# Decay exponentials of a chunked recurrent layer grouped into wider activations, with the split of w moved into the sub-tile loop

## What is computed

```python
w_ = -jnp.exp(w_)                      # decay, from a small projection of h1
wc = jnp.cumsum(w, axis=-2)            # inside chunks of 32 tokens
kw = k * jnp.exp(wc[..., -1:, :] - wc)
S  = S * d[..., None] + kv             # state, chunk after chunk
qe = q * jnp.exp(wc - w)
ke = k * jnp.exp(-wc)
A  = jnp.where(mask, qe @ ke.T, 0.0)
o  = o_inter + A @ v + diag[..., None] * v
out = (groupnorm(o) * silu(g)) @ o_w.T
h = silu(x @ wg.T) * (x @ wu.T); ffn = h @ wd.T
```

## Time and profile before

| | us |
|---|---|
| median of 5 runs | 4532.4 |
| the runs | 4475.2, 4484.1, 4532.4, 4586.9, 4603.8 |
| the profiled execution, slowest core | 4484.1 |
| its span, first to last instruction, core 2 | 4482.5 |
| outside the span | 1.6 |
| spans of the eight cores | 4436.0 to 4482.5 |

### The profile page before, as it was taken

The page is one execution under the profiler, slowest core; times in us unless marked ns, Lnnn a source line. Parts: engine busy times, 40 slices in busy tenths (PEclk is TensorE's granted clock), DMA queues, the critical chain, the costliest instruction groups (busy, mean ns, idle before and its releaser), DMA issues.

```text
span 4482.5 us, 35856 instructions; the slowest of 8 cores (4436.0 to 4482.5 us)
## 1 busy us (share of the span) xinstructions
PE 2154.6 (48%) x11249; PEld 968.6 (22%) x11424; DVE 1449.0 (32%) x2844; ACT 1423.8 (32%) x1552; POOL 300.7 (7%) x525
## 2 busy tenths in 40 slices
PE   0387224762257621675317752187332873248622
PEld 0132111321123211232102321032111321113211
DVE  0230442314432143321433224331343314523144
ACT  0342423323233332333323333243323323324241
POOL 1010000100001000110001000010000100001000
PEclk9998567985679756887558965598656986569856
DMA  9545004540235302443024420254103541044500
GB/s 156 102 80 93 6 12 83 87 78 5 39 69 87 64 5 52 71 82 54 10 52 71 82 50 10 56 85 77 36 10 66 94 74 26 10 75 76 94 5 15
DMA packets 88440, 257.76 MB, mean 58 GB/s; under 512 B 10206, under 2 KB 10527, under 8 KB 84639
## 3 DMA queue, kind: packets, MB, share of 16 engines
q0 software_dynamic: 83088, 221.82, 29.7%
q1 hardware_dynamic: 5168, 33.62, 3.4%
...
## 4 chain that ended last, share of the span: by engine, by line
PEldq 21%; DVE 20%; issue 16%; DMA 14%; ACT 11%; PEld 7%; ACTq 5%; another core or an unknown queue 3%; DVEq 2%; POOL 1%; POOLq 0%; SPq 0%
PEldq L285 20%; ACT L146 10%; DMA sb_fu<-w_fu 7%; ACTq L151 5%; DVE sb_qg L146 4%; DMA sb_x<-x 4%; DMA sb_vgo<-w_g 3%; DVE sb_z L146 3%; DVE sb_gst L146 2%; DVE sb_S L146 2%; DVE sb_o L146 2%; DVE sb_xin L146 1%; DVEq L144 1%; PEld Po L741 1%
## 5 line engine op out<-in xcount | busy, mean ns | idle before, releaser
L146 ACT ACT_TABLE_LOAD x704 | 903.2, 1283 | 3022.7 <-PEq L285 2100.7
L1180 PE MATMUL PtrT<-sb_id,sb_z 128*128 128x128 bf16 x256 | 32.4, 306 | 660.3 <-DVEq L151 660.3
L407 PE MATMUL PtrT<-sb_id,sb_xnt 128*128 128x128 bf16 x256 | 32.4, 306 | 513.1 <-DVEq L151 373.9
L146 DVE COPY sb_gff<-PtrT 128x512 bf16<-128x512 bf16 x64 | 27.2, 425 | 738.4 <-PEq L285 738.4
L577 PE MATMUL Pa<-sb_xnT,sb_fg 128*128 128x512 bf16 x738 | 191.9, 402 | 81.4 <-DMA sb_fu<-w_fu 36.0
L577 PE MATMUL Psm<-sb_xnT,sb_fg 128*128 128x512 bf16 x752 | 178.0, 378 | 61.8 <-DMA sb_fu<-w_fu 37.2
L146 DVE SCALAR_TENSOR_TENSOR sb_hall<-Pb,sb_scr 128x512 bf16<-128x512 f32 x96 | 66.4, 692 | 435.8 <-ACTq L151 431.3
L459 PE MATMUL Pb<-sb_hall,sb_fd 128*128 128x512 bf16 x746 | 201.3, 431 | 9.8 <-issue 9.0
L557 POOL DMA_DIRECT2D sb_fg<-w_fg x192 | 108.9, 567 | 1439.6 <-PEq L285 1400.5
L146 DVE TENSOR_SCALAR sb_qg<-sb_qe,sb_G 128x32 bf16<-128x32 bf16 x768 | 179.9, 234 | 74.4 <-ACTq L151 10.2
L459 PE MATMUL Pa<-sb_hall,sb_fd 128*128 128x512 bf16 x750 | 192.3, 416 | 9.6 <-issue 9.0
...
## 6 DMA issues: line engine op xcount, KB each, us to landing
sb_fg<-w_fg POOLq DMA_DIRECT2D x192, 256.0 KB, 4.0
sb_fu<-w_fu POOLq DMA_DIRECT2D x192, 256.0 KB, 4.8
...
```

The costliest lines, as they stand in the source:

```text
L146: return fn(*a, **k)
L407: e.transpose(Ptr[:, c * 128:(c + 1) * 128], sb_xnt[:, 0, c * 128:(c + 1) * 128], sb_id[:])
L1180: e.transpose(Ptr[:, c * 128:(c + 1) * 128], sb_z[:, c * 128:(c + 1) * 128], sb_id[:])
```

## The change

Four things are done together.

1. The five argument groups of a sub-tile become three. G1 holds qe and kw: 16 matmuls into Pw, one exponential of 1024 columns into sb_ex, two products. G2 holds qt and ks in the same way, through Pab, one tensor that joins Pa and Pb. K holds ke alone (its exponential has the other sign): 8 matmuls into Pa and 512 columns into sb_scr. sb_ex doubles in size.
2. G1 waits for `Supd`, the end of the state update, because that update reads Pw; K waits for G2's exponential, which reads Pab.
3. The w matmul, exponential and split of a sub-tile (`rA`) are no longer made for all four ahead of the stage. That of sub-tile 0 stands there, that of ts + 1 between `rC1(ts)` and `rC2(ts)`. The halves lie in sb_whi and sb_wlo, one sub-tile at a time, and use only Pb and sb_scr.
4. The select becomes a memset of sb_mt and a predicated copy onto it; sb_zero goes.

```diff
-    sb_ex = A("sb_ex", [128, 2, NH * 128], BF16)
+    sb_ex = A("sb_ex", [128, 2, 2 * NH * 128], BF16)
...
-    Pa = nc.alloc_psum_tensor("Pa", [128, 512], F32)
-    Pb = nc.alloc_psum_tensor("Pb", [128, 512], F32)
+    Pab = nc.alloc_psum_tensor("Pab", [128, 1024], F32)
+    Pa = Pab[:, 0:512]
+    Pb = Pab[:, 512:1024]
...
         rB1(it, 0)
         rB2(it, 0)
         for ts_ in range(NST):
             rC1(it, ts_)
+            if ts_ + 1 < NST:
+                rA(it, s, m, ts_ + 1)
             rC2(it, ts_)
             if ts_ + 1 < NST:
                 rB1(it, ts_ + 1)
...
+    def rA(it, s, m, ts_):
+        def pw2_t(e, en, ts_=ts_):
+            en.w(cs, ev["h1"])
+            en.w(cs, st["qk_free"])
+            en.w(cs, st["pb_free_s"])
+            if ts_ > 0:
+                en.w(cs, st["argB_free"])
+            e.matmul(Pb[:, 0:512], sb_h1[:, ts_ * 128:(ts_ + 1) * 128],
+                     sb_ww2[:, :], start=True, stop=True)
+            ev[f"w2t{ts_}"] = sig_t(e)
+        on("tensor", pw2_t)
...
+        def pw2_s(e, en, ts_=ts_):
+            en.w(ct, ev[f"w2t{ts_}"])
+            if ts_ == 0:
+                en.w(ct, ev[f"gft{NC-1}"])
+            else:
+                en.w(cv, ev[f"facK_{ts_-1}"])
+            e.activation(out=wf_ap, in_=Pb[:, 0:512], func=AF.Exp)
+            ev[f"wexp{ts_}"] = sig(e, cs)
+        on("scalar", pw2_s)
...
+        def pw2_v(e, en, ts_=ts_):
+            en.w(cs, ev[f"wexp{ts_}"])
+            if ts_ > 0:
+                en.w(ct, ev[f"gt{ts_-1}"])
+            e.tensor_copy(out=sb_whi[:].rearrange("p h t -> p (h t)"), in_=wf_ap)
+            e.tensor_tensor(out=sb_wlo[:].rearrange("p h t -> p (h t)"),
+                            in0=wf_ap,
+                            in1=sb_whi[:].rearrange("p h t -> p (h t)"),
+                            op=ALU.subtract)
+            ev[f"wsp{ts_}"] = sig(e, cv)
+        on("vector", pw2_v)
...
+        def pG1_t(e, en, ts_=ts_):
+            en.w(cv, ev[f"wsp{ts_}"])
+            en.w(cv, st["Supd"])
+            if ts_ == 0:
+                en.w(cs, ev["pvg4_3"])
+            for h in range(NH):
+                e.matmul(Pw[:, h * 128:(h + 1) * 128], sb_whi[:, h, :],
+                         sb_mqe[:], start=True, stop=False,
+                         skip_group_check=True)
+                e.matmul(Pw[:, h * 128:(h + 1) * 128], sb_wlo[:, h, :],
+                         sb_mqe[:], start=False, stop=True,
+                         skip_group_check=True)
...
+            ev[f"argG1_{ts_}"] = sig_t(e)
+        on("tensor", pG1_t)
...
+        def pG1_s(e, en, ts_=ts_):
+            en.w(ct, ev[f"argG1_{ts_}"])
+            en.w(cv, st["exp_rd"][0])
+            e.activation(out=sb_ex[:, 0, :], in_=Pw[:, :], func=AF.Exp,
+                         bias=0.0, scale=-1.0)
+            ev[f"gx1_{ts_}"] = sig(e, cs)
+        on("scalar", pG1_s)
...
+        def pG2_t(e, en, ts_=ts_):
+            en.w(cv, ev[f"wsp{ts_}"])
+            if ts_ == 0:
+                en.w(cs, st["pa_free_s"])
+                en.w(cs, st["pb_free_s"])
+            else:
+                en.w(cs, ev[f"gxK_{ts_-1}"])
+            en.w(cs, ev[f"wexp{ts_}"])
+            for h in range(NH):
+                e.matmul(Pab[:, h * 128:(h + 1) * 128], sb_whi[:, h, :],
+                         sb_mqt[:], start=True, stop=False,
+                         skip_group_check=True)
...
+        def pG2_s(e, en, ts_=ts_):
+            en.w(ct, ev[f"argG2_{ts_}"])
+            en.w(cv, st["exp_rd"][1])
+            e.activation(out=sb_ex[:, 1, :], in_=Pab[:, :], func=AF.Exp,
+                         bias=0.0, scale=-1.0)
+            ev[f"gx2_{ts_}"] = sig(e, cs)
...
+        def pK_t(e, en, ts_=ts_):
+            en.w(cs, ev[f"gx2_{ts_}"])
+            for h in range(NH):
+                e.matmul(Pa[:, h * 128:(h + 1) * 128], sb_whi[:, h, :],
...
+            ev[f"argK_{ts_}"] = sig_t(e)
+        on("tensor", pK_t)
...
+        def pK_s(e, en, ts_=ts_):
+            en.w(ct, ev[f"argK_{ts_}"])
+            e.activation(out=sb_scr[:, 0:512], in_=Pa[:, :], func=AF.Exp,
+                         bias=0.0, scale=1.0)
+            ev[f"gxK_{ts_}"] = sig(e, cs)
+        on("scalar", pK_s)
...
-            e.select(out=sb_mt[:].rearrange("p h t -> p (h t)"), mask=sb_sel[:],
-                     on_true=Pmt[:, :], on_false=sb_zero[:], add_drain=True)
+            e.memset(sb_mt[:].rearrange("p h t -> p (h t)"), 0.0)
+            e.copy_predicated(out=sb_mt[:].rearrange("p h t -> p (h t)"),
+                              mask=sb_sel[:], data=Pmt[:, :])
```

More of the change, by code:

```diff
@@ L236, in build_program @@
     sb_sg = A("sb_sg", [128, D], F32)
-    sb_zero = A("sb_zero", [128, NH * 128], BF16)
     wf_ap = sb_scr[:].bitcast(F32)
@@ L821, in emit_megatile @@
         on("tensor", ppd_t)
-        wf2_ap = sb_z[:].bitcast(F32)
-        whi4 = [sb_xin[:, 1, w, :] for w in range(NST)]
-        wlo4 = [sb_xin[:, 1, NST + w, :] for w in range(NST)]
-        st["whi4"] = whi4
-        st["wlo4"] = wlo4
-        for wts in range(NST):
-            bank = Pa if wts % 2 == 0 else Pb
-            def pw2_t(e, en, wts=wts, bank=bank):
-                en.w(cs, ev["h1"])
-                if wts == 0:
-                    en.w(cs, st["pa_free_s"])
-                elif wts == 1:
-                    en.w(cs, st["pb_free_s"])
-                else:
-                    en.w(cs, ev[f"wexp{wts-2}"])
-                e.matmul(bank[:, 0:512], sb_h1[:, wts * 128:(wts + 1) * 128],
-                         sb_ww2[:, :], start=True, stop=True)
-                ev[f"w2t{wts}"] = sig_t(e)
-            on("tensor", pw2_t)
-            def pw2_s(e, en, wts=wts, bank=bank):
-                en.w(ct, ev[f"w2t{wts}"])
-                if wts == 0:
-                    en.w(ct, ev[f"gft{NC-1}"])
-                elif wts == 1:
-                    en.w(ct, st.get("z_rd_t", 0))
-                else:
-                    en.w(cv, ev[f"wsp{wts-2}"])
-                wf = wf_ap if wts % 2 == 0 else wf2_ap
-                e.activation(out=wf, in_=bank[:, 0:512], func=AF.Exp)
-                ev[f"wexp{wts}"] = sig(e, cs)
-            on("scalar", pw2_s)
-            def pw2_v(e, en, wts=wts):
-                en.w(cs, ev[f"wexp{wts}"])
-                if wts == 0:
-                    en.w(ct, projev[3])
-                wf = wf_ap if wts % 2 == 0 else wf2_ap
-                e.tensor_copy(out=whi4[wts], in_=wf)
-                e.tensor_tensor(out=wlo4[wts], in0=wf, in1=whi4[wts],
-                                op=ALU.subtract)
-                ev[f"wsp{wts}"] = sig(e, cv)
-            on("vector", pw2_v)
-        ev["wspall"] = ev[f"wsp{NST-1}"]
-        st["argA_free"] = ev["wexp2"]
-        st["argB_free"] = ev["wexp3"]
-        if f"whi_{it}" in dumps:
-            def pwhid(e, en):
-                en.w(cv, ev["wsp0"])
-                e.tensor_copy(out=sb_whi[:].rearrange("p h t -> p (h t)"),
-                              in_=whi4[0])
-                ev["whid"] = sig(e, cv)
-            on("vector", pwhid)
-            dump(f"whi_{it}", sb_whi, cv, ev["whid"])
+        rA(it, s, m, 0)
         rB1(it, 0)
@@ new lines, in rA @@
+    def rA(it, s, m, ts_):
[30 more added lines that the diff above has]
+        if ts_ == 0:
+            dump(f"whi_{it}", sb_whi, cv, ev["wsp0"])
@@ L960, in pg_t @@
         def pg_t(e, en, ts_=ts_):
-            en.w(cv, ev["wspall"])
+            en.w(cv, ev[f"wsp{ts_}"])
             en.w(cv, st.get("psm_rd", 0))
@@ L964, in pg_t @@
                 en.w(cs, ev[f"gs{ts_-1}"])
-            whi = st["whi4"][ts_]
-            wlo = st["wlo4"][ts_]
             for h in range(NH):
-                e.matmul(Psm[:, h * 8:(h + 1) * 8],
-                         whi[:, h * 128:(h + 1) * 128], sb_pm[:],
+                e.matmul(Psm[:, h * 8:(h + 1) * 8], sb_whi[:, h, :], sb_pm[:],
                          start=True, stop=False)
-                e.matmul(Psm[:, h * 8:(h + 1) * 8],
-                         wlo[:, h * 128:(h + 1) * 128], sb_pm[:],
+                e.matmul(Psm[:, h * 8:(h + 1) * 8], sb_wlo[:, h, :], sb_pm[:],
                          start=False, stop=True)
@@ L1261, in p0_v @@
         def p0_v(e, en):
-            e.memset(sb_zero[:], 0.0)
             e.memset(sb_S[:].rearrange("p h v -> p (h v)"), 0.0)
```

122 lines of the change are left out of this document (76 added, 46 removed).

## The result

The changed kernel takes 4507.5 us in the median of 43 runs (4478 to 4661); the kernel before, now with 80 runs, 4485.4 us. The ratio is 1.0044, 95% interval 1.0029 to 1.0060: about 20 us slower, with 13 and 27 as the ends. That is within the 2% called no change, but clear of the noise of so many runs. In some executions the cores of one die show a lower granted clock and the time is some per cent longer; all ratios here are of the executions without that, so they are not quite the quotients of the medians. The profiled execution took 4499.0 us, of which the slowest core's span is 4497.5.

The account below looks back on a forecast made before the run. No engine is near full; chains of hand-overs bound the kernel. Head -7.56, hand-overs +10.29, select +0.76, splits +0.60 make +4.09 us per megatile, +33 us: 4517 by the profiled run, 4565 by the median; predicted 4540, range 4470 to 4610.

Parts of the forecast that it names:

- The sum: Recurrent stage, per megatile: -7.56 head, +10.29 hand-overs, +0.76 select, +0.60 splits, +4.09 us; times 8, +33 us.
- the two waits of VectorE for TensorE: VectorE waiting for po_t and the output projection; only the splits' +4.8 us counted at po_t, no clock change.
- Head of the stage: From the end of the first w split to the first sb_qg scaling: 12.04 us against 19.60, 7.56 us gained per megatile.
- Hand-over: End of state update to the reduction of sb_o: 14.41 against 10.98 us, 3.43 lost, three times per megatile.
- Select: Memset of sb_mt 0.485 us against the zeros copy's 0.294: +0.19 us each, +0.76 us per megatile.
- The splits inside the loop: Next sub-tile's w work between select and update: 0.32 us in about 15 of 24 places, 0.60 us per megatile.
- VectorE's idle before the reduction should rise from 108.0 to about 190: Sign to check: idle before the sb_o reduction rises by 24 x 3.4 us, with the wait on ScalarE.
- the low clock: Rival: TensorE stays at 1.2 GHz through the whole recurrent stage, +94 us, 4578 us; chance 0.10.
- The high clock: Rival: G1 and G2's 32 matmuls raise TensorE's clock; projection saves 65 us, po_t 15, giving 4408 us; chance 0.08.
- The free wait: Rival: G1's wait for Supd costs nothing and the saved loads count in full, -114 us, 4370 us; chance 0.04.
- the case with the chance of 0.86: Whole kernel: time within 2% of the kernel before, from the forecast's 0.78 plus the high clock's 0.08.

Follow-up runs that it names:

- e2: Changed kernel with all four w exponentials and splits ahead of the recurrent stage again; ratio 1.0133 to the kernel before.
- e5: Kernel before, with only a wait added: the first argument group also waits for the end of the state update (Supd); ratio 1.028.
- e3: Changed kernel with the banks of G1 and G2 exchanged, so G2 waits for the update and K for G1's exponential; ratio 0.984 to the kernel before.
- e1: Kernel before with the select alone changed to a memset and a predicated copy; one execution, 4480.0 us.
- e9: Changed kernel plus 8 filler matmuls of 512 columns into Po, starting with the square root's result; ratio 1.0019 to the kernel before.
- e4: e3 with K also placed ahead of G2 on all three engines; ratio 0.981 to the kernel before.
- e8: e4 with the square right behind G1's exponential, G behind the square root, and the 24 sb_qg scalings behind the sb_ogT copy; ratio 0.923 to the kernel before.

## Why the prediction was right or wrong

**The step that failed is the last one: "I predict between, 4540 us."** The sum was made against the profiled execution (4484.1), and the predicted time was then moved halfway to a median of five runs (4532.4), of which two were far above the others. With 80 runs that median is 4485.4. Against the 4532.4 then shown, 4540 says "nothing happens" (+0.2%); against 4485.4 it says +55 us (+1.2%), over twice what was measured. The sum itself said +33 us, +0.7%. The measured +0.44% is clear of zero and on the sum's side. 4484.1 + 33 = 4517 would have been the number to give; measured were 4507.5.

**Inside the sum, the step that failed is the two waits of VectorE for TensorE.** They were put at +4.8 us (the splits) and, for the clock, at nothing; they measured -12.6. The mechanism of the change itself, a shorter head paid for by a longer hand-over, was right.

The terms, in the order of the prediction:

- Head of the stage: 7.56 us gained by the working, 7.8 measured (62.1 / 8). Right. e2 shows its parts, which the working had not separated: 6.3 us by the splits, 1.5 by the grouping. This was where table loads on the path were saved, and it is the smaller part.
- Hand-over: +3.43 by the working, 78.1 / 24 = +3.25 measured. Right in cause and nearly in size. e5 puts the wait on the kernel before and gets 15.71 for 15.7; e3 takes it from G1, and K's wait for G2 with it, and gets 10.74 for 10.8.
- Select: +0.19 each, right (e1), but the memset also starts some 0.13 us later than the copy did, about 4 us in all that the sum had at nothing. The memset took 0.485 us every time, so the halved form of the Trainium skill (VectorE: DVE Perf Modes, "Zero memsets can be issued as uint32 (trn2)") was not used for sb_mt. The page's rule that it costs by the element agrees with the trace: 0.912 for 1024 columns, 0.485 for 512.
- "The splits inside the loop", +0.60 us per megatile: wrong. e2 has no split there and the stretch is 0.4 us shorter in all, over 24 places. The rows of the changed kernel behind its select of sub-tile 1 in the fourth megatile:

```profile
2172.07 0.43 DVE L146 CAST sb_whi<-sb_scr 128x512 bf16<-128x512 f32 x1 [0.27 <-ACTq L151]
2172.58 0.69 DVE L146 TENSOR_TENSOR sb_wlo<-sb_scr,sb_whi 128x512 bf16<-128x512 f32 x1
2173.65 1.41 DVE L146 TENSOR_SCALAR sb_z<-sb_v,Psm 128x256 bf16<-128x256 bf16 x4 [0.38 <-PEq L285]
```

The split is over at 2173.27 and VectorE still waits 0.38 us for po_t, although that runs at the full clock. The working had VectorE wait some 0.8 us for the w exponential, and it waited 0.27. (Its count was off too: the 8 waits of sub-tile 3 are all short and have no split, so 12 of the 24 are short and not 15.)
- TensorE's clock was not in the sum. The waits for po_t and the projection fell by 12.6 us (262.4 to 249.8). Two places make some 10 of that, and in both the granted clock inside the stretch rose: po_t of sub-tile 1 (2.61 us at 0.72 to 1.97 at 0.97) and the projection behind sub-tile 0 (6.37 at 0.63 to 5.77 at 0.68), eight times each. e1, where the order on TensorE is that of the kernel before, has 2.62 and 6.37 there. The rest is within what e1 shows as scatter. That the clock is what shortened them is shown by these figures; what in the new order raised it stays open, and e9, which was to test it, did not move it.
- "VectorE's idle before the reduction should rise from 108.0 to about 190": wrong, it is 109.3. The amount was right, the place was not. Idle is counted in front of each instruction, and the products that used to lie under the update moved in between.

The rivals: the low clock (+94 us) did not come here; part of it came in e4 and e8. The Trainium skill (TensorE: Matmul & The Clock Gate, "HAM oscillation"), by which bursts shorter than the waits between them begin at the half clock, agrees with the 0.56 and 0.50 of the two bursts above, but the stage as a whole did not slow down by it: over the recurrent stage of the second megatile the granted clock is 0.61, where it was 0.59. The high clock (-80 in the two waits) came at about a sixth of its size. The free wait is refuted by e5.

The range of 4470 to 4610 held the time, and the case with the chance of 0.86 is the one that came. That the sum's +33 lies as near to the measured +20 as it does is partly luck. The five stretches of the stage add up to +9.4 us where the sum had +32.7, the memset's later start adds 4, and the other 12.4 are in the stretch between stages, where nothing was edited. With them the stretches give +26; the medians of the eight core spans differ by 23.5. What lies between the +13 of the stage and the +20 of the runs, whose interval reaches down to 13, stays open.
